# Cross-attention and mixture of experts on one core: experts as three float32r products, weights split by GpSimd into a ring of four, token rows scattered once

## The chip, the cores and the metric

One of the eight cores of a Trainium2 chip runs the whole program. A core has TensorE (PE; its weight loads are listed apart as PEld), VectorE (DVE), ScalarE (ACT), GpSimd (POOL), SyncE (SP), 16 DMA engines, SBUF with 128 partitions, and eight PSUM banks of 128 x 512 float32. The metric is the device time of one execution in microseconds, as the median of several runs. A granted clock of 1.0 is TensorE's 2.4 GHz, 0.5 its 1.2 GHz.

## The reference

There are 32 sequences of 64 tokens with 512 values each, all float32; the work goes by tiles of 128 tokens (two sequences), 16 of them.

```python
x = x + xattn(layernorm(x), ctx, ctx)   # autocorrelation attention, 8 heads, top 8 lags
x = x + moe(layernorm(x))

def moe(x):                             # per token
    g, u = split(x @ shared_w_gate_up.T)            # 512 -> 2 x 512
    shared = (silu(g) * u) @ shared_w_down.T        # 512 -> 512
    p = softmax(x @ gate_w.T)                       # 16 experts
    w, idx = top_k(p, 2);  w = w / sum(w)
    # every chosen expert: g, u = split(x @ w_gate_up[e].T)   512 -> 2 x 128
    #                      y_e  = (silu(g) * u) @ w_down[e].T 128 -> 512
    return sum_k w[k] * y_idx[k] + shared
```

A token goes to two experts, so there are 4096 pairs of token and expert. Each expert's pairs are filled up to whole tiles of 128 "slots". 47 tiles are always worked on, which is enough for any routing; those after the last filled one are done with expert 15.

## The kernel before, in words

Every engine has its own instruction stream, written out in order, and semaphores between them. In time order:

**Attention** (to about 203 us). Sixteen pairs of sequences go through a software pipeline: forward transforms as products with constant matrices (the context as three float32r products, `split_product`, L453), products, top lags, inverse, the sum into `resid`, the second normalisation `x2n`, its transposes, which are kept in `x2T`, and the gate's logits. SP loads `x` and `ctx` and stores `x2n` to DRAM (`x2_rows`, L405); every second pair it loads two experts' gate/up weights (`load_expert_pair`, L394), so that all of them stand in SBUF (`wgu_sb`).

**Routing and shared group 0** (to about 249 us). DVE ranks the logits and computes the slot of every pair (`pos_i`, L1043). To turn this into a list of tokens by slot (`slot_token`) and weights by slot (`slot_w`), DVE and GpSimd build one-hot matrices in eight turns (L1061 and L1235), and TensorE multiplies them (`slots`, L612). Between these, TensorE does group 0 (four token tiles) of the shared expert in float32 (`shared_half`, `shared_down`).

**The experts** (about 249 to 403 us). For slot tile `j`, GpSimd copies 128 indices and gathers 128 rows of `x2_rows` with an indirect DMA (`gather`, L1244). TensorE transposes them (L643), ScalarE copies them out of PSUM (L814), and TensorE multiplies by the expert's gate and up weights, in float32, at an address read from a table (L655): 128 x 256, four blocks. ScalarE takes the SiLU (L822), DVE multiplies with up and with the slot's weight (L1086), TensorE turns the activation (L664), DVE copies it (L1083), TensorE multiplies by the down weights (L670), DVE copies the result (L1091), and SP stores it to `y_rows` in DRAM. In iteration `j` TensorE's order is gate/up of `j`, transposes of `j+1`, the turn of `j-1`, the down product of `j-2`. The loops are hardware loops (`Fori`).

**Shared groups 1 to 3** (about 403 us to the end). Their operands are split in two float32r halves (`hi` by ScalarE, `lo` as the difference by DVE), and each product is done as hi x hi + hi x lo + lo x hi (`split_half`, L571; `split_down`, L586): 96 and 48 products of 512 columns per group. Meanwhile, once every `y` is stored (L1263), GpSimd gathers the results back by token: 16 tiles, two choices each, in four turns of eight buffers (`gather_results`, L1270). DVE adds them to `resid` (`add_results`, L1101), in one order with its multiplies and splits for TensorE, and adds the shared result (`shared_add`, L1007). A buffer is gathered into again when its last content has been added (`y_added`). SP stores each finished tile of `resid`.

Of the kernel before, what the change touches and what calls it, by code (L numbers as in the profile page):

```python
# [42 lines left out]
E = 16  # L43
# [5 lines left out]
JW = SLOT_TILES + 1  # L49
GROUPS = 4  # L50
# [5 lines left out]
HOTS = 4  # L56
HOT_TURNS = CHOICES * PAIRS // HOTS
# [84 lines left out]
def build(nc, x, ctx, consts, gate, w_gu, w_down, sh_gu, sh_down, out):  # L142
    with ExitStack() as stack:
# [3 lines left out]
        def in_turn(name, width, later):  # L147

            with nc.sbuf_tensor(name, [P, width], F32) as first:
                pass  # L150
            spare = width - sum(w for _, w, _ in later)
            tenants = [sb(n, [P, w], dt) for n, w, dt in later]
            if spare:
                sb(name + "_spare", [P, spare])
            return first, tenants
# [17 lines left out]
        x2_rows = nc.dram_tensor("x2_rows", [TOKENS, D], F32, kind="Internal").ap()  # L173
        y_rows = nc.dram_tensor("y_rows", [SLOT_TILES * P, D], F32, kind="Internal").ap()
# [4 lines left out]
        for name, width in CONSTANTS:  # L179
# [6 lines left out]
        wgu_sb, (y_in_low, shgu_hi, shgu_lo, tokens_hi, tokens_lo, act_lo) = in_turn("wgu_sb", E * KB * 2 * INTER, [  # L186
            ("y_in_low", YBUFS // 2 * D, F32), ("shgu_hi", KB * 2 * SHARED, F32R), ("shgu_lo", KB * 2 * SHARED, F32R),
            ("tokens_hi", GT * D, F32R), ("tokens_lo", GT * D, F32R), ("act_lo", SB * D, F32R)])
        shgu_sb = sb("shgu_sb", [P, KB * 2 * SHARED])
        gate_sb = sb("gate_sb", [P, KB * E])  # L190

        arena, (shd_hi, shd_lo, act_hi) = in_turn("arena", 21 * D, [
            ("shd_hi", SB * D, F32R), ("shd_lo", SB * D, F32R), ("act_hi", SB * D, F32R)])
        xg_sb = sb("xg_sb", [P, 2 * D])
        silu_sb = sb("silu_sb", [P, D])
        b_at = [0]
# [7 lines left out]
        ctx_halves = (act_lo[:, 0:D], act_lo[:, D:2 * D])  # L204
        matrices_halves = (act_lo[:, 2 * D:2 * D + 2 * P], act_lo[:, 2 * D + 2 * P:2 * D + 4 * P])
# [14 lines left out]
        wd_sb = arena[:, 0:E * D]  # L220
        shd_sb = arena[:, E * D:(E + SB) * D]
        totals = arena[:, (E + SB) * D:(E + SB) * D + E * PAIRS]
        cumul = arena[:, (E + SB) * D + E * PAIRS:(E + SB + 1) * D]


        EARLY_DOWN = (E - SB) * D
        sh_act = arena[:, EARLY_DOWN:EARLY_DOWN + SB * D]
# [7 lines left out]
        xgT = [x2T[:, 0:D], x2T[:, D:2 * D]]  # L235
        y_out = [x2T[:, 2 * D:3 * D], x2T[:, 3 * D:4 * D]]
        xg = [xg_sb[:, 0:D], xg_sb[:, D:2 * D]]
        act_sb = sb("act_sb", [P, P])
        actT_both = sb("actT_both", [P, 2 * P])
        actT_sb = [actT_both[:, 0:P], actT_both[:, P:2 * P]]  # L240

        y_in = [(y_in_low if i < YBUFS // 2 else x2T)[:, i % (YBUFS // 2) * D:(i % (YBUFS // 2) + 1) * D] for i in range(YBUFS)]
# [32 lines left out]
        hilo_i = sb("hilo_i", [P, CHOICES * PAIRS], I32)  # L275
        hi_f = sb("hi_f", [P, CHOICES * PAIRS])
        lo_f = sb("lo_f", [P, CHOICES * PAIRS])
        tile_e = sb("tile_e", [P, JW])

        tile_gu_at, tile_down_at = sb("tile_gu_at", [P, JW], I32), sb("tile_down_at", [P, JW], I32)  # L280

        lane_hot = [xg_sb[:, k * HOTS * P:(k + 1) * HOTS * P] for k in range(2)]
        tile_hot = [const_sb[:, k * HOTS * 2 * JW:(k + 1) * HOTS * 2 * JW] for k in range(2)]
        slot_token = sb("slot_token", [P, JW], I32)
        slot_w = sb("slot_w", [P, JW])
# [5 lines left out]
        ps_xgT, ps_gu, ps_y, ps_actT = bank[0], bank[6:8], bank[3:5], bank[5]  # L291
        ps_gate, ps_up, ps_shared = (bank[1], bank[7]), bank[2], (bank[0], bank[5], bank[3], bank[4])
        ps_slots, ps_rank, ps_total = bank[6], bank[3], bank[4]
# [4 lines left out]
        gate_loaded, wgu_loaded, shgu_loaded = sem("gate_loaded"), sem("wgu_loaded"), sem("shgu_loaded")  # L298
        wd_loaded, shd_loaded = sem("wd_loaded"), sem("shd_loaded")
# [24 lines left out]
        lane_hot_ready, tile_hot_ready = sem("lane_hot_ready"), sem("tile_hot_ready")  # L324
        slots_psum, slots_ready = sem("slots_psum"), sem("slots_ready")
        tile_hot_found = sem("tile_hot_found")
        tile_e_ready, pos_ready = sem("tile_e_ready"), sem("pos_ready")
# [5 lines left out]
        gidx_ready = sem("gidx_ready")  # L333
        gathered = [sem("gathered0"), sem("gathered1")]
        xgT_psum, xgT_ready, gu_psum, silu_ready = sem("xgT_psum"), sem("xgT_ready"), sem("gu_psum"), sem("silu_ready")
        act_ready, actT_psum, actT_ready = sem("act_ready"), sem("actT_psum"), sem("actT_ready")
        down_psum, y_ready = sem("down_psum"), sem("y_ready")
# [21 lines left out]
        WEIGHT_BLOCKS = [(i % 2, i // 2) for i in range(1, 2 * SB)] + [(0, 0)]  # L359
# [25 lines left out]
        def _(sp):  # L385
# [8 lines left out]
            def load_expert_pair(h):  # L394
                width = 2 * KB * 2 * INTER
                sp.dma_start(wgu_sb[:, bass.ds(h * width, width)],
                             w_gu[:, bass.ds(h * width, width)]).then_inc(wgu_loaded, 16)

            def iteration(h, b, n):
                if live(n, 2) and n != -2:  # L400
                    load_pair(h + 1, b)
                if live(n, -2):
                    p, pb = pair(h, b, -2)
                    sp.wait_ge(x2n_ready, p + 1)
                    sp.dma_start(x2_rows[bass.ds(p * P, P), :], x2n[pb]).then_inc(x2_stored[pb], 16)  # L405
                if n == 2:
                    sp.dma_start(shgu_sb[:, :], sh_gu[:, :]).then_inc(shgu_loaded, 16)
                if b == 1 and (n is None or 1 <= n < PAIRS):

                    wait(sp, wgu_loaded, 16 * h)  # L410
                    if n == PAIRS - 1:
                        sp.wait_ge(ctx_odd_psum, PAIRS)
                    load_expert_pair(h)
# [8 lines left out]
            sp.wait_ge(logits_psum, PAIRS)  # L422
            sp.wait_ge(x2T_kept, PAIRS)
            for b in range(2):
                sp.wait_ge(x2_stored[b], 16 * PAIRS // 2)
            sp.dma_start(shd_sb, sh_down[:, :]).then_inc(shd_loaded, 16)
            sp.dma_start(wd_sb[:, 0:EARLY_DOWN], w_down[:, 0:EARLY_DOWN]).then_inc(wd_loaded, 16)
            for t in range(GT):
                sp.wait_ge(sh_out_psum, t + 1)
                cols = slice(EARLY_DOWN + t * D, EARLY_DOWN + (t + 1) * D)  # L430
                sp.dma_start(wd_sb[:, cols], w_down[:, cols]).then_inc(wd_loaded, 16)

            def store_y(h, b):
                j = 2 * h + b
                sp.wait_ge(y_ready, j + 1)
                sp.dma_start(y_rows[bass.ds(j * P, P), :], y_out[b]).then_inc(y_stored[b], 16)

            with sp.Fori(0, SLOT_TILES // 2) as h:
                for b in range(2):
                    store_y(h, b)  # L440
# [873 lines left out]
```

## Time and profile before

| | |
|---|---|
| median of 3 runs | 509.45 us (509.12 to 509.93) |
| span of the profiled execution | 507.2 us |
| TensorE busy | 476.8 us (94%) |
| VectorE, ScalarE, GpSimd busy | 312.2, 222.7, 227.3 us |
| DMA | 66.76 MB, 132 GB/s over the span |

The only time of the profiled execution itself is its span, from its first to its last instruction; the runs' times hold in addition what lies around the span, and their median is 2.25 us above it. A busy time counts a matmul from its start to its modelled end, so neighbours overlap in it; the distance between starts tells the pace. The name behind an instruction is the tile that it writes, then those that it reads. "idle before, releaser" says how long an engine had nothing to do ahead of a group and what ended that.

### The profile page before, as it was taken

Reading aid. Unit: us, or ns where it says so; the run is one execution under the profiler, and the core shown is the slowest. Engines: PE = TensorE matmul, PEld = TensorE weight load, DVE = VectorE, ACT = ScalarE, POOL = GpSimd, SP = SyncE. Lnnn points to the kernel's source line nnn. Section 1 sums busy time; section 2 is a strip of 40 time slices with the busy share of each in tenths; the row PEclk is TensorE's granted clock in tenths of the full one; section 3 lists DMA queues with packets and bytes.
Section 4 is the critical chain, followed back from the end, with each engine's and each line's share of the span. In section 5 each row is a group of like instructions: output and inputs, shape, how many; then the busy total and the mean of one; then the engine's idle time right before and its main releaser. Section 6 shows DMA issues by size and latency. Waiting matters only on the chain.

```text
span 507.2 us, 8574 instructions
## 1 busy us (share of the span) xinstructions
PE 476.8 (94%) x2097; PEld 328.1 (65%) x2098; DVE 312.2 (62%) x972; ACT 222.7 (44%) x425; POOL 227.3 (45%) x384
## 2 busy tenths in 40 slices
PE   4789999999999999898899999999999999999997
PEld 2556556656655655356576667766667678888885
DVE  3799899999999863884133333333333566747643
ACT  4778888888888835200122222122221435022120
POOL 2356676676667544044333333333333026466520
PEclk9899999999999999999999999999999999999999
DMA  4416533424253031801435555455554314555622
GB/s 157 163 43 237 173 110 127 145 63 146 68 180 114 36 103 43 331 0 43 124 113 157 165 165 151 150 158 161 165 153 151 131 63 126 159 174 165 207 62 83
DMA packets 24923, 66.76 MB, mean 132 GB/s; under 512 B 3456, under 2 KB 3456, under 8 KB 23488
## 3 DMA queue, kind: packets, MB, share of 16 engines
q1 hardware_dynamic: 18576, 45.74, 25.0%
q0 software_dynamic: 6320, 20.71, 15.6%
q8 instruction: 11, 0.18, 0.1%
q14 instruction: 16, 0.13, 0.1%
HBM read 45.73 MB, written 20.71 MB: 131 GB/s over the span
## 4 chain that ended last, share of the span: by engine, by line
PE 62%; DVE 15%; POOL 8%; issue 8%; ACT 5%; DMA 1%; SPq 0%; DVEq 0%; POOLq 0%; ACTq 0%
PE bank L457 19%; PE bank L655 17%; PE bank L670 8%; PE bank L643 4%; DVE top_v L923 4%; POOL arena L1198 4%; PE bank L469 4%; POOL arena L1201 4%; PE bank L558 2%; DVE arena L928 2%; PE bank L567 2%; DVE stats L886 2%; DVE resid L911 2%; ACT arena L772 2%; ACT arena L771 2%
## 5 line engine op out<-in xcount | busy, mean ns | idle before, releaser
L655 PEld LDWEIGHTS bank<-wgu_sb,x2T 128*128 128x128 f32 x376 | 67.6, 189 | 41.0 <-issue 33.6
L655 PE MATMUL bank<-wgu_sb,x2T 128*128 x376 | 92.0, 388 | 2.1 <-ACT x2T L814 0.6
L814 ACT COPY x2T<-bank 128x512 f32<-128x512 f32 x47 | 27.5, 585 | 142.6 <-PE bank L643 142.6
L1251 POOL DMA_INDIRECT xg_sb<-x_rows,gidx x47 | 45.9, 976 | 98.0 <-PE bank L643 93.6
L1083 DVE COPY actT_both<-bank 128x128 f32<-128x128 f32 x47 | 13.7, 291 | 73.3 <-PE bank L664 73.3
L670 PE MATMUL bank<-arena,actT_both 128*128 x94 | 47.9, 593 | 0.0
L457 PE MATMUL bank<-act_lo 128*128 128x512 f32 x96 | 41.2, 538 | 6.7 <-DVE act_lo L965 6.7
L457 PE MATMUL bank<-tokens_hi,shgu_hi 128*128 128x512 f32 x92 | 36.2, 394 | 0.0
L457 PE MATMUL bank<-tokens_hi,shgu_lo 128*128 128x512 f32 x92 | 35.8, 389 | 0.0
L457 PE MATMUL bank<-tokens_lo,shgu_hi 128*128 128x512 f32 x92 | 35.8, 389 | 0.0
L457 PEld LDWEIGHTS bank<-act_lo 128*128 128x128 f32 x96 | 18.7, 197 | 22.8 <-issue 20.8
L558 PE MATMUL bank<-x2T,shgu_sb 128*128 128x512 f32 x72 | 32.6, 596 | 0.4 <-DVE arena L882 0.4
L1091 DVE COPY x2T<-bank 128x512 f32<-128x512 f32 x47 | 32.0, 680 | 0.8 <-PE bank L670 0.8
L1086 DVE SCALAR_TENSOR_TENSOR act_sb<-bank,slot_w,silu_sb 128x128 f32<-128x128 f32 x47 | 16.4, 350 | 23.8 <-ACT silu_sb L822 23.8
L643 PE MATMUL bank<-const_sb,xg_sb 128*128 128x128 f32 x188 | 28.3, 272 | 1.7 <-DMA xg_sb<-x_rows,gidx 1.7
L481 PE MATMUL bank<-const_sb,arena 128*128 128x128 f32 x128 | 26.0, 286 | 3.1 <-DVE arena L897 3.1
L1198 POOL TENSOR_TENSOR arena<-arena 128x512 f32<-128x512 f32 x16 | 20.5, 1284 | 18.1 <-ACT arena L772 18.1
L1201 POOL TENSOR_TENSOR arena<-arena 128x512 f32<-128x512 f32 x16 | 20.3, 1271 | 18.5 <-DVE arena L953 18.3
L481 PEld LDWEIGHTS bank<-const_sb,arena 128*128 128x128 f32 x128 | 21.5, 201 | 10.9 <-issue 7.8
L643 PEld LDWEIGHTS bank<-const_sb,xg_sb 128*128 128x128 f32 x188 | 23.5, 140 | 7.6 <-issue 3.1
L719 ACT ACTIVATE silu_sb<-bank 128x512 f32<-128x512 f32 x16 | 9.6, 598 | 40.1 <-PE bank L457 28.7
L882 DVE TENSOR_TENSOR arena<-bank,silu_sb 128x512 f32<-128x512 f32 x16 | 11.1, 691 | 26.0 <-PE bank L457 24.9
(153 smaller groups left out, 1077.7 us busy)
## 6 DMA issues: line engine op xcount, KB each, us to landing
y_rows<-x2T SPq DMA_DIRECT2D x47, 256.0 KB, 3.1
wgu_sb<-w_gu SPq DMA_DIRECT2D x8, 1024.0 KB, 5.3
resid<-x SPq DMA_DIRECT2D x16, 256.0 KB, 2.8
arena<-ctx SPq DMA_DIRECT2D x16, 256.0 KB, 3.3
x_rows<-arena SPq DMA_DIRECT2D x16, 256.0 KB, 2.1
result<-resid SPq DMA_DIRECT2D x16, 256.0 KB
arena<-w_down SPq DMA_DIRECT2D x1, 3072.0 KB, 13.0
shgu_sb<-sh_gu SPq DMA_DIRECT2D x1, 2048.0 KB, 8.0
```

The costliest lines, as they stand in the source:

```text
L457: last = mm(ps, a[i], b[k], start=start and n == 0, stop=stop and n == len(terms) - 1)
L469: mm(ps_out[:, :], C["out_odd"], odd_prod, start=False, stop=True).then_inc(out_psum, 1)
L481: mm(ps_corr[:, cols], prod_plain[:, cols], C["corr_plain"], start=True, stop=False)
L558: last = mm(ps[:, :].rearrange("p (t n) -> p t n", t=GT), shgu_sb[:, col:col + P], shared_tokens(g, c), start=c == 0, stop=c == KB - 1)
L643: last = nc.tensor.transpose(ps_xgT[:, cols], xg[b][:, cols], C["identity"])
L655: last = mm(ps_gu[b][:, 0:2 * INTER], xgT[b][:, c * P:(c + 1) * P], wgu_sb[:, bass.ds(at + c * 2 * INTER, 2 * INTER)], start=c == 0, stop= ...
L670: mm(ps_y[b][:, :], actT_sb[b], wd_sb[:, bass.ds(at, D)], start=True, stop=True).then_inc(down_psum, 1)
L814: copy(xgT[b], ps_xgT[:, :]).then_inc(xgT_ready, 1)
L1091: nc.vector.tensor_copy(y_out[b], ps_y[b][:, :]).then_inc(y_ready, 1)
L1198: nc.gpsimd.tensor_tensor(w_odd_sw, w_odd_sw, ctx_odd_im[pb], ALU.mult).then_inc(odd_im_products, 1)
L1201: nc.gpsimd.tensor_tensor(odd_prod, odd_prod, w_odd_sw, ALU.add).then_inc(odd_product_ready, 1)
L1251: nc.gpsimd.indirect_dma_start(xg[b], None, x2_rows[:, :], bass.IndirectOffsetOnAxis(ap=gidx[b][:, 0:1], axis=0)).then_inc(gathered[b], 16)
```

## The change

1. **Expert products in float32r.** The expert weights are one array now (gate/up and down of an expert side by side, 1536 columns). GpSimd loads one expert at a time into one of two raw buffers, copies it to a float32r `hi` and subtracts for `lo`, into one of four ring slots. `expert_split` counts the experts that are ready; a slot is used again when the tiles of the expert four before are done (`expert_tiles` against `expert_free`). Tokens by slot and activations are split too: `hi` by ScalarE, `lo` by DVE. Gate/up of a tile is 12 products of 256 columns, down three of 512. Transposes run two tiles ahead, into two banks; ScalarE copies the result `y`. The loops are written out.
2. **Rows are scattered once.** Instead of one-hot products and a gather per tile, SP loads the 16 tiles of `x2_rows` again, GpSimd scatters each twice by `pos_i` to a DRAM array in slot order (`x_slots`, 32 indirect DMAs), and SP loads a slot tile with a plain DMA. During attention SP fills `x_slots` with zeros (47 stores), since some slots stay empty. No slot tile is loaded, and no expert is split, before every scatter has landed.
3. **Order.** Shared group 1 is done before the experts; its weights' `lo` halves and its tokens' are GpSimd's work, ahead of the scatter, and ScalarE makes the `hi` halves between group 0's SiLUs. Four of the row buffers lie where `act_lo` will be, so DVE's first multiply of group 1 waits for their scatters. Group 2 starts behind the last tiles.
4. **Weights of the two choices** are applied when the results are added (`scalar_tensor_tensor`), and those additions stand elsewhere in DVE's order: the first turn after group 2's multiplies, the second with group 2's shared additions, the third in group 3's loop, the fourth behind it.

The core of the diff:

```diff
+            for t in range(PAIRS):                       # SP
+                if t == ROWS_LOW:
+                    sp.wait_ge(sh_up_psum, SB)
+                    sp.wait_ge(weights_lo_ready, 2 * SB)
+                if t >= ROWS_LOW + ROWS_HIGH:
+                    sp.wait_ge(rows_scattered[t - ROWS_HIGH], 16 * CHOICES)
+                sp.dma_start(row_buffer(t), x2_rows[t * P:(t + 1) * P, :]).then_inc(rows_loaded[t], 16)
...
+            for t in range(PAIRS):
+                sp.wait_ge(rows_scattered[t], 16 * CHOICES)
+            for j in range(SLOT_TILES + 6):
+                if j < SLOT_TILES:
+                    load_slots(j)
+                if j >= 6:
+                    store_y(j - 6)
...
+            def gate_up(j):                              # TensorE
+                at = weights_at(j)
+                need = pe.value_load(tile_need[0:1, j:j + 1], min_val=1, max_val=E)
+                pe.wait_ge(xgT_lo_ready, j + 1)
+                pe.wait_ge(expert_split, need)
+                for c in range(KB):
+                    last = split_product(ps_gu[j % 2][:, 0:2 * INTER],
+                                         of_halves(xgT_halves[j % 2], lambda x: x[:, c * P:(c + 1) * P]),
+                                         of_expert(at, c * 2 * INTER, 2 * INTER), c == 0, c == KB - 1)
+                last.then_inc(gu_psum, 1)
...
+            for j in range(SLOT_TILES):
+                gate_up(j)
+                if j + 2 < SLOT_TILES:
+                    transposes(j + 2)
...
+                if j >= 1:
+                    turn_act(j - 1)
+                if j >= 2:
+                    down(j - 2)
...
+            for t in range(PAIRS):                       # GpSimd
+                if t == PAIRS // 2:
+                    pool.wait_ge(sh_up_psum, SB)
+                    pool.wait_ge(tokens_lo_ready, GT)
+                    load_raw(0)
+                    load_raw(1)
+                pool.wait_ge(rows_loaded[t], 16)
+                for k in range(CHOICES):
+                    nc.gpsimd.indirect_dma_start(x_slots[:, :], bass.IndirectOffsetOnAxis(ap=pos_i[:, k * PAIRS + t:k * PAIRS + t + 1], axis=0),
+                                                 row_buffer(t), None).then_inc(rows_scattered[t], 16)
+
+            def split_expert(e):
+                pool.wait_ge(raw_loaded[e % 2], 16 * (e // 2 + 1))
+                hi, lo = (slot(e)[:, half * EXPERT:(half + 1) * EXPERT] for half in range(2))
+                nc.gpsimd.tensor_copy(hi, raw[e % 2]).then_inc(expert_hi, 1)
+                rest(lo, raw[e % 2], hi, expert_split, expert_hi, e + 1)
+                if e + 2 < E:
+                    pool.wait_ge(expert_split, e + 1)
+                    load_raw(e + 2)
...
+            for e in range(E):
+                if e == 2:
+                    pool.wait_ge(sh_out_psum, 2 * GT)
+                if e >= RING:
+                    pool.wait_ge(expert_tiles, pool.value_load(expert_free[0:1, e - RING:e - RING + 1], min_val=1, max_val=SLOT_TILES + 1))
+                    apart(pool, pool_passed)
+                split_expert(e)
...
+            slots_lo(0)                                  # DVE
+            slots_lo(1)
+            shared_add(1, 2)
+            shared_add(1, 3)
+            for j in range(SLOT_TILES):
+                expert_multiply(j)
+                if j + 2 < SLOT_TILES:
+                    slots_lo(j + 2)
+                if j >= 1:
+                    expert_act_lo(j - 1)
```

## Rows read from the trace of the kernel before

**Rows 1.** Busy time by stage: DMA share and GB/s last.
```profile
249.50:403.00 153.50, 151.35 (x694) 107.53 (x693) 56.44 (x138) 35.93 (x94) 50.87 (x87) 1.00 0.50 152
438.40:507.20 68.80, 65.40 (x289) 53.83 (x287) 36.44 (x55) 11.83 (x20) 29.11 (x45) 1.00 0.47 147
```
**Rows 2.** Timeline of TensorE: start, us, instruction; first gate/up, two tiles later on.
```profile
249.48 3.62 PE L655 MATMUL bank<-wgu_sb,x2T 128*128 x16
...
320.69 1.99 PE L655 MATMUL bank<-wgu_sb,x2T 128*128 x8
322.51 0.60 PE L643 MATMUL bank<-const_sb,xg_sb 128*128 128x128 f32 x4
322.95 0.27 PE L664 MATMUL bank<-const_sb,act_sb 128*128 128x128 f32 x1
323.06 1.02 PE L670 MATMUL bank<-arena,actT_both 128*128 x2
323.92 1.94 PE L655 MATMUL bank<-wgu_sb,x2T 128*128 x8
...
327.32 1.99 PE L655 MATMUL bank<-wgu_sb,x2T 128*128 x8
```
**Rows 3.** Timeline of TensorE, first and last of 48 float32r down products.
```profile
427.48 0.39 PE L457 MATMUL bank<-shd_hi,act_hi 128*128 128x512 f32 x1
...
438.13 0.39 PE L457 MATMUL bank<-shd_hi,act_lo 128*128 128x512 f32 x1
```
**Rows 4.** Timeline of TensorE, the logits: products of 16 columns.
```profile
177.97 0.96 PE L502 MATMUL bank<-gate_sb,xg_sb 128*128 128x16 f32 x8
```
**Rows 5.** Groups by form: busy us, mean ns of one, idle before them.
```profile
L814 ACT COPY x2T<-bank 128x512 f32<-128x512 f32 x47 | 27.5, 585 | 142.6 <-PE bank L643 142.6
L1229 POOL TENSOR_TENSOR act_lo<-arena,act_lo 128x512 fp32r<-128x512 f32 x15 | 19.0, 1268 | 12.2 <-ACT act_lo L739 12.2
L1192 POOL COPY x2T<-xg_sb 128x512 f32<-128x512 f32 x15 | 9.2, 614 | 0.0
```
**Rows 6.** Timeline of DVE: slot positions, and the last multiply of group 0.
```profile
216.44 0.18 DVE L1043 CAST pos_i<-pos_f 128x32 int32<-128x32 f32 x1
...
223.70 0.69 DVE L882 TENSOR_TENSOR arena<-bank,silu_sb 128x512 f32<-128x512 f32 x1
```
**Rows 7.** Timeline of GpSimd, gathers of results: first two, ninth, last of 32.
```profile
414.99 0.97 POOL L1280 DMA_INDIRECT y_in_low<-y_rows,gidx  x1 [3.08 <-issue]
...
416.98 0.97 POOL L1280 DMA_INDIRECT y_in_low<-y_rows,gidx  x1 [0.81 <-POOL gidx L1275]
...
435.26 1.24 POOL L1280 DMA_INDIRECT y_in_low<-y_rows,gidx  x1 [3.54 <-DVE resid L1112]
...
485.14 1.30 POOL L1280 DMA_INDIRECT x2T<-y_rows,gidx  x1 [0.83 <-POOL gidx L1275]
```
**Rows 8.** DMA queues: packets, MB, share; issues: count, KB, us to landing.
```profile
q1 hardware_dynamic: 18576, 45.74, 25.0%
q0 software_dynamic: 6320, 20.71, 15.6%
...
resid<-x SPq DMA_DIRECT2D x16, 256.0 KB, 2.8
...
xg_sb<-x_rows,gidx POOLq DMA_INDIRECT x47, 3.7
```
**Rows 9.** Busy time near the start; TensorE first, granted clock third from last.
```profile
16.00:18.00 2.00, 0.09 (x1) 0.00 (x0) 2.00 (x16) 1.96 (x5) 0.00 (x0) 1.00 0.42 95
18.00:20.00 2.00, 1.20 (x5) 1.21 (x6) 2.00 (x6) 1.94 (x5) 0.28 (x1) 0.68 1.06 400
20.00:22.00 2.00, 2.00 (x12) 2.00 (x11) 0.32 (x2) 0.47 (x1) 1.84 (x6) 0.50 0.70 274
```
**Rows 10.** Timeline of DVE: the last copied y, and the last sum.
```profile
408.94 0.69 DVE L1091 COPY x2T<-bank 128x512 f32<-128x512 f32 x1
...
503.84 0.69 DVE L1010 TENSOR_TENSOR resid<-bank,resid 128x512 f32<-128x512 f32 x1 [2.03 <-PE bank L457]
```

More of the change, by code:

```diff
@@ L49 @@
 JW = SLOT_TILES + 1
+RING = 4
+EXPERT = KB * 2 * INTER + D
+DOWN = KB * 2 * INTER
+SLOT = 2 * EXPERT
+ROWS_LOW, ROWS_HIGH = 4, 8
 GROUPS = 4
@@ L145, in sb, with over @@
             return stack.enter_context(nc.sbuf_tensor(name, shape, dt))
[L147 to L155, printed above, removed]
+        def over(tenants):
+            held = ExitStack()
+            made = [held.enter_context(nc.sbuf_tensor(n, [P, w], dt)) for n, w, dt in tenants]
+            held.close()
+            return made
         sems = {}
@@ L626, in _ @@
             shared_half(0, 3, 1)
[L627 removed]
             pe.wait_ge(shd_loaded, 16)
             shared_down(0, 0)
[L630 removed]
             shared_down(0, 1)
[L632 to L640 removed]
+            pe.wait_ge(pos_ready, 1)
+            shared_down(0, 2)
+            shared_down(0, 3)
@@ L641, in transposes @@
+            for i, (part, m) in enumerate(WEIGHT_BLOCKS):
+                pe.wait_ge(weights_lo_ready, i + 1)
+                split_half(1, m, part)
+            def transposes(j):
+                pe.wait_ge(xg_loaded[j % 2], 16 * (j // 2 + 1))
+                wait(pe, xgT_lo_ready, j - 1)
                 for c in range(KB):
                     cols = slice(c * P, (c + 1) * P)
-                    last = nc.tensor.transpose(ps_xgT[:, cols], xg[b][:, cols], C["identity"])
+                    last = nc.tensor.transpose(ps_xgT[j % 2][:, cols], xg[j % 2][:, cols], C["identity"])
@@ L699, in _, with weights_at, of_expert @@
-            pe.wait_ge(weights_lo_ready, len(WEIGHT_BLOCKS) + SB)
-            pe.wait_ge(xgT_ready, SLOT_TILES)
-            pe.wait_ge(actT_ready, SLOT_TILES)
-            pe.wait_ge(y_ready, SLOT_TILES)
-            split_down(1)
-            with pe.Fori(2, GROUPS) as g:
+            def weights_at(j):
+                return pe.value_load(tile_at[0:1, j:j + 1], min_val=0, max_val=(RING - 1) * SLOT)
+            def of_expert(at, first, width):
+                return tuple(ring[:, bass.ds(at + (half * EXPERT + first), width)] for half in range(2))
@@ L1093, in _ @@
-            for n in range(2):
-                expert(0, n, n)
-            with dve.Fori(1, SLOT_TILES // 2) as h:
-                for b in range(2):
-                    expert(h, b, None)
-            expert(SLOT_TILES // 2, 0, SLOT_TILES - 1)
             def add_results(quad, u):
@@ L1167, in _ @@
                 split_act_lo(3, m)
-                add_results(3, m)
+                add_results(2, m)
+            for t in range(GT):
+                add_results(3, t)
             dve.wait_ge(y_added, PAIRS)
@@ L1254, in _, with rest @@
-            pool.wait_ge(slots_ready, 1)
-            for b in range(2):
-                pool.wait_ge(x2_stored[b], 16 * PAIRS // 2)
-                gather(0, b)
-            with pool.Fori(1, SLOT_TILES // 2) as h:
-                for b in range(2):
-                    gather(h, b)
-            gather(SLOT_TILES // 2, 0)
+            def rest(dst, src, hi, done, hi_ready, value):
+                pool.wait_ge(hi_ready, value)
+                nc.gpsimd.tensor_tensor(dst, src, hi.bitcast(F32), ALU.subtract).then_inc(done, 1)
```

496 lines of the change are left out of this document (219 added, 277 removed).

## The prediction

> **What bounds the kernel now.** I read the stages first, then one expert tile, then the three resources that the change leans on: GpSimd, the DMA engines, and what follows the last expert tile. In the stage of the experts TensorE is busy for 151 of 153.5 us and in the last stage for 65.4 of 68.8 [rows 1]; the other engines are at a third or less, DMA at about half. So both stages are bound by TensorE. A tile starts every (327.32 - 320.69)/2 = 3.32 us [rows 2]: 1.82 for the eight gate/up instructions, 0.44 for four transposes, 0.11 for turning the activation, 0.86 for the down product; that is 3.23, and the rest is a pause ahead of every second tile, where the gate/up waits for ScalarE's copy of the transposes made just before it. The end of the kernel is a TensorE chain too: DVE's last sum starts at 503.84 and runs 0.69, and 2.7 us of storing later the span is over [rows 10]. GpSimd's 32 gathers of results run beside it from 414.99 to 485.14 [rows 7] and cost nothing now.
>
> **Expert products.** A float32r product of 512 columns starts every (438.13 - 427.48)/47 = 0.227 us [rows 3]. No 256-column one is in the trace. Half of that, 0.113, is its lower bound (what an instruction costs besides its columns can only add), the full 0.227 its upper one. A weight load with a 16-column product behind it takes at most 0.96/8 = 0.12 [rows 4], so the load alone sets about the same floor, and I take 0.12. Gate/up is then 12 x 0.12 = 1.44, down 3 x 0.227 = 0.68, the transposes stay at 0.44 and 0.11: 2.67. Transposes now run two tiles ahead, which removes the pause; I leave 0.05 for the rest: 2.72 a tile, with ends of 2.64 and 4.0. For the 47 tiles TensorE needs 47 x 1.49 + 45 x 0.44 + 46 x 0.11 + 45 x 0.68 = 125.5 us, then two group-2 halves of 12 x 0.227 and the two last downs, 6.9, and ScalarE's copy of the last result, 0.6 [rows 5]: the last y stands 133.0 us after the first gate/up.
>
> What must keep up with 2.72: ScalarE has 2 x 0.585 for transposes and y [rows 5] and two narrower operations, at most as much again: 2.34. GpSimd splits an expert in 3 x 0.614 + 3 x 1.268 = 5.65, issues one load and waits a little: 6.9, or 7.7 if an issue costs 1.8. The inputs' routing, counted from the reference, fills 42 of the 47 tiles, so an expert lasts 42/16 x 2.72 = 7.1; with a ring of four and the last seven or eight tiles all at expert 15, even 7.7 delays the end by 2 us at most. DMA moves two 256 KB blocks a tile at 126.8/45.74 us per MB (the q1 row, 0.73 a block) and 0.79 MB of weights per expert, 0.83 a tile [rows 8]: 2.28 of 2.72, tight but within.
>
> **What goes before the experts.** The 32 one-hot products between the downs go, their DVE and GpSimd halves too, and so do the 47 gathers by GpSimd. pos_ready still comes at 216.6, the last up of group 0 is read from 223.7, its activation stands at 224.4 [rows 6]; four downs of four 0.86 products [rows 2] then end group 0 at 238.2, where the experts start at 249.5 now. Group 1 follows at once: 96 products of 0.227 to 260.0, plus 1.4 for a new wait (DVE's first multiply of the group stands behind the landing of four scattered tiles at about 247, and the up of block 1 waits for it), then 24 more: 266.8. Here TensorE runs dry, because the experts wait for the scatter. GpSimd splits the shared weights and tokens first: the tokens wait for that last up and a ScalarE copy of 0.6, to 224.1, and eight subtractions of 1.268 end at 234.3. Then 32 scatters and two loads are queued on it, and every expert split stands behind them. One issue costs at least its own 0.97 and at most 0.97 + 0.83, for each gather now starts 0.81 to 0.83 after what released it [rows 7]. I take that the 0.83 passes beside the issue before, since a scatter, other than a gather, waits for no index copy. Then DMA decides: a software-queue DMA holds all 16 engines for 79.1/79 = 1.0 us [rows 8], so 32 scatters, four row tiles (2.9) and two raw experts (4.4) need 39.3 us, 1.16 an issue. From 235.1 they are issued by 274.4, and landed 2.7 later (3.7 from issue to landing), at 277.1. SP's first slot load takes 2.8, as its x tiles do [rows 8]: 279.9. TensorE has then been idle for 13 us. Near the start, after two microseconds with 0.09 busy, the granted clock was 0.68 and then 0.50 (the lower of its two levels, 1.2 of 2.4 GHz) in stretches of 2 us [rows 9]; I take the loss of those, 0.64 + 1.0 = 1.7. Two transposes and 24 products are 6.3: the first gate/up at 287.9. Expert 0 is split by 277.1 + 5.7, earlier. So the experts start 38.4 us later, and of these only 144 x 0.227 = 32.7 are group 1, done ahead: the hole eats more than the dropped one-hots gave.
>
> **What comes after.** The last y stands at 287.9 + 133.0 = 420.9, against 408.94 + 0.69 = 409.63 now. So the loop gives 27.1 and the last y is still 11.3 later. Groups 2 and 3 alone would let TensorE end at 480 (288 x 0.227 from 413.4, and 1.5 for the last tiles). But the gathers start only when every y is stored: 5.36 after the last y [rows 7, 10], at 426.3. Their code is unchanged: 70.15 us from the first issue to the last, 3.54 of it a wait that won't recur, so 66.6, to 492.9, and 3.7 to land: 496.6. What was hidden becomes the end. DVE adds one result (0.7) and four shared sums (2.5), and 2.7 us of storing follow the last one [rows 10]: 502.5. From the last y to the end it is 81.6 us instead of 97.6. On the way TensorE waits for DVE, because the group-3 multiply stands behind the additions of the second turn of gathers (to about 463); that is inside the gathers' time and costs nothing.
>
> **Other edits.** 47 zero stores (34 us of DMA time) replace eight weight loads of 1 MB (23) over the 180 us of attention, where DMA is busy for under half: nothing, at most a late context tile or two, 0 to 5. Routing steps cut on DVE: 2 us, not on the path. ScalarE's splits of the shared weights between SiLUs: under group 0's products. Weights applied in the last additions instead of per tile: the additions keep their 0.7.
>
> **Sum.** Span 507.2 - 4.7 = 502.5. The median of the runs is 509.45, 2.25 above the profiled span; so 504.8.
>
> **A rule against it.** The Trainium skill, "TensorE: Matmul & The Clock Gate", Part 3, has LDWEIGHTS overlapping a running matmul only where the row groups differ. Rows 3 speak against that: load and 512 columns together take 0.227. At 256 columns it is the third rival below.
>
> **The rivals.** *Issues at 1.8* (ends slower): if the 0.83 can't overlap, 34 issues take 61.2, the landing is at 299.0 instead of 277.1, and all behind it moves: 526.7 with the 2.25. It decides from 1.30 us an issue on, where the 4.7 are gone. For it: every gather shows it. Against: what stands before each gather is a dependent copy. *The tile is not cheaper*: 256-column products at 0.16, because of register-addressed operands, late slot loads at 84% DMA or the splits' pace, give 3.2 a tile, +22.5: 527. For it: no such product has run; against: float32 instructions of 256 columns take half of those of 512. *Loads in series with the products*: 0.12 + 0.113 each, +1.36 a tile, +64: 569. *Cheaper queue*: scatters at 0.97 and DMA no limit (-5), the 3.08 us before the first gather gone: 497. *Gathers don't bind*: only if they sped up by a third; TensorE sets the end, 480 + 3.4 + 2.25: 486.
>
> **How the numbers follow.** Forecast 0.45 (own range 500 to 510), issues at 1.8 0.21, dear tile 0.17, loads in series 0.03, cheaper queue 0.10, gathers that don't bind 0.04. About 0.2% is what a measurement can tell, 508.4 to 510.5. Faster: 0.36 of the 0.45, 0.10 and 0.04, together 0.50. Same: 0.06. Slower: the rest, 0.44. For eight in ten I go from the cheaper queue, 494, to the two rivals at 527, 529.
>
> **What would show it.** Right: gate/up groups of about 1.45 us at 2.7 us a tile; a hole in TensorE from about 267 to 280, released by a slot load, with the lower clock behind it; first gate/up near 288; gathers some 2.06 us apart as the last chain, with TensorE done over 10 us before the end. Wrong: scatters 1.8 apart; tiles above 3 us; the chain at the end on TensorE; expert_split as what releases the gate/up.

## The result: 562.3 us, slower by 10.2%

The changed kernel takes 562.26 us (median of 4 runs, 559.76 to 564.59), the kernel before 509.69 beside it (4 runs): a ratio of 1.102 [1.097, 1.106]. The forecast was 504.8, the range 494 to 529: outside it, and on the other side of no change. The profiled span is 562.8 us against a forecast span of 502.5, 60.3 more. That execution took 564.6 us, 2.3 above the median. Two runs of the experiments below fell into a slower state (683.5 us without reads, 504.0 with one load for two tiles): the ratios leave them out, and the medians without them are 519.9 and 498.9. Three marks of the trace divide these 60.3:

| mark | forecast | measured | of it new here |
|---|---|---|---|
| first gate/up starts | 287.9 | 294.82 | +6.9 |
| last y copied (from the first gate/up on) | 420.9 (133.0) | 478.45 (183.6) | +50.6 |
| end (from the last y on) | 502.5 (81.6) | 562.8 (84.4) | +2.8 |

So five sixths of the miss lie inside the expert loop. The first mark itself moves between executions: in the kernels below whose start is unedited it lies between 292.6 and 294.8, so of the +6.9 some 2 are spread.

### The profile after, stage by stage

Busy time of the two last stages, which answers [rows 1]: the expert tiles up to the last copied y, then the rest.

```profile
294.80:478.45 183.65, 150.28 (x961) 124.44 (x960) 55.57 (x141) 75.46 (x188) 77.03 (x42) 0.99 0.53 184
478.45:562.80 84.35, 61.38 (x262) 49.98 (x260) 40.88 (x59) 11.03 (x20) 42.81 (x64) 0.88 0.50 153
```

TensorE, the first engine in the row, was busy for 151.35 of 153.5 us in the experts before; now it is busy for 150.3 of 183.7, at full clock (0.99), and no other engine comes to half (the DMA engines' share is 0.53). Something that is not a listed instruction fills 33 us.

One tile, which answers [rows 2]: the timeline of all engines from a down product to the next gate/up.

```profile
402.34 0.72 PE L467 MATMUL bank<-ring,actT_hi 128*128 x2
...
402.90 0.39 PE L467 MATMUL bank<-ring,actT_lo 128*128 x1
...
403.11 0.69 DVE L1095 TENSOR_TENSOR xgT_lo<-bank,xgT_hi 128x512 fp32r<-128x512 f32 x1 [0.46 <-ACT xgT_hi L835]
...
404.01 0.32 PEld L467 LDWEIGHTS bank<-ring,xgT_hi 128*128 128x128 f32 x2 [1.14 <-issue]
404.01 0.51 PE L467 MATMUL bank<-ring,xgT_hi 128*128 x2 [0.73 <-DVE xgT_lo L1095]
...
404.36 0.28 PE L467 MATMUL bank<-ring,xgT_lo 128*128 x1
...
404.72 0.28 PE L467 MATMUL bank<-ring,xgT_lo 128*128 x1
```

The previous gate/up started at 400.30, so a tile takes 3.7 here and 3.80 on average over three (the next starts are 407.85 and 411.69), not 2.72. From 404.36 to 404.72 there are three products: 0.12 each, as forecast. The down products start 0.23 to 0.28 apart; 402.90 is the third, and behind it the next product was due at 403.13. What is new is the 0.88 from 403.13 to 404.01. The row of PE puts the wait down to DVE's `xgT_lo`, and so does the chain of waits (start, us, what):

```profile
402.01 0.45 PE bank L652 x4
402.46 0.02 issue
402.49 0.60 ACT xgT_hi L835
403.08 0.02 issue
403.11 0.70 DVE xgT_lo L1095
403.81 0.20 issue
404.01 1.71 PE bank L467 x12
```

This is theory C (chain): transposes, ScalarE's half, VectorE's rest, next gate/up. But the code speaks against it. The rest that DVE makes at 403.11 is for the transposes of 402.01, two tiles ahead; the gate/up of 404.01 needs the one that was made a tile earlier. The row of the weight loads says something else: 1.14 of "issue", time in which nothing that the profile shows was waited for. The trace also has what TensorE's own sequencer did meanwhile: the register instructions of its stream, listed as PEldq under the lines that read registers (ns as min/median/max, then first and last start). A read is a load of a register from a table in SBUF, an operation on it and an assertion that it lies within its bounds. L656 is the place of the weights, L664 the count of split experts:

```profile
L656 PEldq TENSOR_LOAD <-tile_at x1: 301/301/301, 402.5 to 402.5; - x1
L656 PEldq FUSED_REGOPS  x1: 151/151/151, 402.8 to 402.8; - x1
L656 PEldq SEQ_ASSERT  x1: 18/18/18, 403.1 to 403.1; - x1
...
L664 PEldq TENSOR_LOAD <-tile_need x1: 297/297/297, 403.1 to 403.1; - x1
L664 PEldq FUSED_REGOPS  x1: 151/151/151, 403.5 to 403.5; - x1
L664 PEldq SEQ_ASSERT  x1: 18/18/18, 403.7 to 403.7; - x1
```

The two reads run one after the other from 402.5 to 403.7, 0.6 us each with the steps between; a third, for the down product, stands at 401.5. Meanwhile only down products that stand ahead of them in the stream still start (the last at 402.90), and gate/up starts right behind them. This is theory R (reads): 1.8 us a tile on the sequencer, with only 2.7 us of products to cover them.

The start of the experts, which answers the bounds from [rows 7] and the clock of [rows 9]: GpSimd's second, third and last scatter (the first stands at 238.98), and then TensorE.

```profile
240.51 0.97 POOL L1248 DMA_INDIRECT x_slots<-rows_low,pos_i  x1 [0.30 <-issue]
241.79 0.96 POOL L1248 DMA_INDIRECT x_slots<-rows_low,pos_i  x1 [0.30 <-issue]
...
281.34 0.96 POOL L1248 DMA_INDIRECT x_slots<-shgu_sb,pos_i  x1 [0.31 <-issue]
```

```profile
286.70 1.97 PE L652 MATMUL bank<-const_sb,x2T 128*128 128x128 f32 x8 [15.24 <-DMA x2T<-x_slots]
...
288.89 0.63 PE L467 MATMUL bank<-shd_lo,act_hi 128*128 128x512 f32 x1
289.31 0.63 PE L467 MATMUL bank<-shd_hi,act_lo 128*128 128x512 f32 x1
...
294.82 0.40 PE L467 MATMUL bank<-ring,xgT_hi 128*128 x2
```

Most scatters stand 1.27 to 1.28 apart. TensorE stands idle for 15.24 us, released by a slot load, and its products are then 0.42 apart instead of 0.23, the lower of its two clocks, until 290.2 (granted clock 0.50 up to 290, 1.00 from 291).

The end, which answers [rows 7, 10]: first, ninth and the last two gathers of results, then the last two lines of DVE.

```profile
481.54 1.03 POOL L1285 DMA_INDIRECT x2T<-y_rows,gidx  x1 [0.83 <-POOL gidx L1280]
...
501.06 0.98 POOL L1285 DMA_INDIRECT x2T<-y_rows,gidx  x1 [4.00 <-DVE resid L1091]
...
550.13 0.98 POOL L1285 DMA_INDIRECT x2T<-y_rows,gidx  x1 [0.81 <-POOL gidx L1280]
...
552.12 1.15 POOL L1285 DMA_INDIRECT x2T<-y_rows,gidx  x1 [0.81 <-POOL gidx L1280]
```

```profile
555.79 0.75 DVE L1091 SCALAR_TENSOR_TENSOR resid<-x2T,r_w,resid 128x512 f32<-128x512 f32 x1 [1.58 <-DMA x2T<-y_rows,gidx]
556.58 2.48 DVE L1029 TENSOR_TENSOR resid<-bank,resid 128x512 f32<-128x512 f32 x4
```

The last chain runs over the gathers, 2.0 apart, as forecast; TensorE's last product is done near 548.5.

### The profile page after: what moved, and what is told of

It reads as the page before. It is cut to its first block, busy times and chain, and to the rows that moved or that the text cites. A ratio compares the mean times of both kernels' runs of the same rounds, so it can differ in the third digit from the quotient of the medians.

```text
span 562.8 us, 8677 instructions
## 1 busy us (share of the span) xinstructions
PE 465.2 (83%) x2272; PEld 336.3 (60%) x2272; DVE 296.5 (53%) x937; ACT 262.4 (47%) x519; POOL 302.7 (54%) x371
## 4 chain that ended last, share of the span: by engine, by line
PE 33%; POOL 19%; DVE 18%; issue 14%; ACT 9%; DMA 5%; SPq 1%; POOLq 1%; DVEq 0%; ACTq 0%
PE bank L467 20%; POOL x_slots L1248 5%; DVE xgT_lo L1095 5%; ACT xgT_hi L835 4%; POOL x2T L1285 4%; PE bank L652 4%; PE bank L568 4%; DVE top_v L942 3%; POOL arena L1183 3%; POOL arena L1186 3%; PE bank L479 3%; DMA resid<-x 2%; DVE arena L947 2%; DVE stats L905 2%; DVE resid L930 2%
## 5 line engine op out<-in xcount | busy, mean ns | idle before, releaser
L467 PE MATMUL bank<-ring,xgT_hi 128*128 x376 | 75.3, 298 | 31.4 <-DVE xgT_lo L1095 30.6
L467 PEld LDWEIGHTS bank<-ring,xgT_hi 128*128 128x128 f32 x376 | 59.4, 192 | 50.2 <-issue 50.0
L1223 POOL TENSOR_TENSOR ring<-x2T,ring 128x1536 fp32r<-128x1536 f32 x16 | 55.5, 3470 | 1.4
L467 PE MATMUL bank<-ring,xgT_lo 128*128 x188 | 53.6, 285 | 0.0
L1095 DVE TENSOR_TENSOR xgT_lo<-bank,xgT_hi 128x512 fp32r<-128x512 f32 x47 | 32.5, 692 | 38.4 <-ACT xgT_hi L835 38.4
L1285 POOL DMA_INDIRECT x2T<-y_rows,gidx x32 | 34.9, 1091 | 29.7 <-POOL gidx L1280 23.0
L652 PE MATMUL bank<-const_sb,x2T 128*128 128x128 f32 x188 | 29.4, 281 | 16.2 <-DMA x2T<-x_slots 16.2
L835 ACT CAST xgT_hi<-bank 128x512 fp32r<-128x512 f32 x47 | 27.6, 587 | 27.2 <-PE bank L652 27.2
L467 PEld LDWEIGHTS bank<-ring,xgT_lo 128*128 128x128 f32 x188 | 36.3, 193 | 0.0
L467 PE MATMUL bank<-ring,actT_hi 128*128 x94 | 33.9, 442 | 1.0 <-issue 0.8
L652 PEld LDWEIGHTS bank<-const_sb,x2T 128*128 128x128 f32 x188 | 22.6, 145 | 16.8 <-DMA x2T<-x_slots 16.8
```

Of the source, the lines that this page charges most:

```text
L467: last = mm(ps, a[i], b[k], start=start and n == 0, stop=stop and n == len(terms) - 1)
L652: last = nc.tensor.transpose(ps_xgT[j % 2][:, cols], xg[j % 2][:, cols], C["identity"])
L835: copy(xgT_halves[j % 2][0], ps_xgT[j % 2][:, :]).then_inc(xgT_hi_ready, 1)
L1095: tt(dst, src, hi.bitcast(F32), ALU.subtract).then_inc(done, 1)
L1223: nc.gpsimd.tensor_tensor(dst, src, hi.bitcast(F32), ALU.subtract).then_inc(done, 1)
L1285: nc.gpsimd.indirect_dma_start(y_in[buf], None, y_rows[:, :], bass.IndirectOffsetOnAxis(ap=gidx[buf][:, 0:1], axis=0)).then_inc(y_gathered ...
```

## The experiments

All are edits of the changed kernel. The first two write this input's routing into the program, and half the scatter leaves out the rows of the second choices, which only a diagnosis may do. "Loop" is the time from the first gate/up to the last copied y.

| kernel | us | ratio to before | loop |
|---|---|---|---|
| changed kernel | 562.3 | 1.102 [1.097, 1.106] | 183.6 |
| count known | 542.3 | 1.065 [1.062, 1.068] | 162.9 |
| no reads | 520.2 | 1.019 [1.016, 1.022] | 140.3 |
| read early, place used twice | 532.8 | 1.047 [1.043, 1.050] | 151.3 |
| four tiles a read, unbounded | 655.6 | 1.288 [1.283, 1.293] | 276.3 |
| four tiles a read, bounded | 547.3 | 1.076 [1.071, 1.081] | 169.2 |
| one read a tile | 525.8 | 1.033 [1.027, 1.039] | 146.2 |
| direct gathers | 543.0 | 1.066 [1.062, 1.071] | 183.7 |
| half the scatter | 552.3 | 1.083 [1.079, 1.087] | 184.0 |
| one read and direct gathers | 506.8 | 0.994 [0.992, 0.996] | 145.8 |
| the same, late downs first | 502.9 | 0.986 [0.984, 0.988] | 148.4 |
| the same, one load for two tiles | 499.4 | 0.979 [0.975, 0.982] | 142.7 |

### Which waits fill the loop: the count known, no reads

```diff
-                need = pe.value_load(tile_need[0:1, j:j + 1], min_val=1, max_val=E)
+                need = TILE_EXPERT[j] + 1
```

> The count of split experts that a tile waits for is written into the program; the place of the weights is still read, twice a tile. Theory R (reads): TensorE's sequencer spends about 0.6 us on each of its three register reads of a tile (0.30 load, 0.15 register operation, 0.02 assertion and the steps between), and in float32r there is not enough queued work ahead of them. One read of three goes: the loop falls from 3.80 us a tile to about 3.2, 47 x 0.6 = 28 us less, about 534 us. Theory C (chain: transposes, ScalarE's rounded half, VectorE's rest, next gate and up, as the chain of waits shows it): nothing changes, 3.80 us a tile and 562 us.

542.3 us, loop 162.9: 20.8 less, 0.44 a tile. C, which expects no change, falls. R had 0.6 a tile and 534 us: it missed by 8, as if part of the read was covered.

```diff
-                return pe.value_load(tile_at[0:1, j:j + 1], min_val=0, max_val=(RING - 1) * SLOT)
+                return TILE_EXPERT[j] % RING * SLOT
```

> Place and count are both written into the program; TensorE reads no register at all in the loop, and the products, the waits on the data and all other engines stay. Theory R: the loop falls to the 2.72 us a tile that the products need, or up to 2.85 with the waits: 47 x 0.95 to 1.08 = 45 to 51 us less, 511 to 517 us. Theory C: the chain over ScalarE and VectorE stays as long as it is, 3.80 us a tile and 562 us.

The count is a constant here too, and with the place the address of every weight product becomes one: the operation of 0.046 us on the sequencer that makes such an address (shown with the four-tile reads below) goes as well. 520.2 us, loop 140.3: 43.3 less than in the changed kernel, with ScalarE's and VectorE's part untouched. That the reads are what counts, and not the address operations, shows in the last run below: it keeps these, and its loop takes 142.7. TensorE's timeline, three tiles on end, and its waits in the loop (us in total, times, longest):

```profile
399.38 0.40 PE L470 MATMUL bank<-ring,xgT_hi 128*128 128x256 f32 x2
...
402.07 0.40 PE L470 MATMUL bank<-ring,xgT_hi 128*128 128x256 f32 x2
...
404.75 0.39 PE L470 MATMUL bank<-ring,xgT_hi 128*128 128x256 f32 x2
```

```profile
PE bank L655 <- DMA x2T<-x_slots: 7.0, 10, 1.3
```

A tile takes 2.68: the forecast's 2.72 is what the products need once the reads are gone. All that is left of TensorE's waits are ten for slot loads, 7.0 us, which are the 7.3 by which this loop exceeds the forecast 133.0. They can account for the 3 us by which the time ends above R's 511 to 517.

### Place or number of the reads: early, and in one instruction

```diff
             for j in range(SLOT_TILES):
                 gate_up(j)
+                if j + 1 < SLOT_TILES:
+                    read(j + 1)                  # place and count of the next tile
...
             def down(j):
-                at = weights_at(j)
+                at, _ = places.pop(j)            # the register that gate_up used
```

> The two reads for tile j+1 stand right behind the products of gate and up of tile j, ahead of the transposes, and the down product uses the register that gate and up used, so two reads a tile instead of three. Theory R, with the sequencer as the serial resource: the third read goes and the place of the other two does not matter: about 3.2 us a tile, 28 us less, 534 us. Theory R, with only the place at fault (nothing queued behind which to read): 2.72 to 2.85 us a tile, 511 to 517 us. Theory C: 562 us.

532.8 us, loop 151.3: far from what place alone would give (511 to 517), near the serial version (534). But the kernel with the count known also reads twice a tile, and its loop takes 162.9; so the place counts too, by 0.25 us a tile, and neither version holds alone. The number of reads is the larger part: the two that are left still cost 11.0 us beside none.

```diff
+            def read(j, n=4):                    # in gate_up, every fourth tile
+                load = lambda table, **bounds: nc.values_load_multi_w_load_instructions(table[0:1, j:j + n], ..., **bounds)[1]
+                tables = (load(tile_at, skip_runtime_bounds_check_because=...), load(tile_need, min_val=1, max_val=E))
```

> One instruction reads the places of four tiles, one the counts of four tiles; the down product uses the place again. Theory R: two loads of 0.30 and four register operations with assertions of about 0.17 for every four tiles, about 0.4 us a tile instead of 1.8, part of it covered: 2.75 to 3.1 us a tile, 33 to 49 us less, 513 to 529 us. Theory C: 562 us.

655.6 us, 93 more where 33 to 49 less were expected: both theories wrong here, the edit had a cost of its own. The sequencer's rows on the products' line, 40 us of the loop:

```profile
L467 PEldq FUSED_REGOPS  x137: 42/146/168, 381.9 to 420.0; - x137
L467 PEldq SEQ_ASSERT  x102: 18/18/18, 382.1 to 419.5; - x102
```

In the changed kernel the address of a weight product cost an operation of 0.046 and no assertion (from 400 to 408 us):

```profile
L467 PEldq FUSED_REGOPS  x23: 46/46/51, 400.2 to 408.0; - x23
```

Here, where the place was read without bounds, it costs 0.146 and an assertion at every use. With bounds:

> As the kernel that reads four tiles at once, which took 655 us, but the places are read with bounds. Theory: there the trace has a register operation of 0.15 and an assertion of 0.02 for the address of every weight product instead of an operation of 0.046, because a value without bounds is asserted at each use; with bounds these go and the eight assertions for four tiles come in one piece, about 2.0 us for every four tiles: 2.9 to 3.2 us a tile, 520 to 535 us. Rival: one instruction that fills four registers is itself slow: it stays near 655 us.

547.3 us, loop 169.2, 107 less: bounds were the cause. It missed 520 to 535 by 12. The eight operations of four tiles come in one piece: nine waits of TensorE whose only releaser in the profile is "issue" hold 18.1 us in the loop, the longest 2.2. And the granted clock is lower, 0.92 on average between 300 and 420 against 0.99 in the changed kernel (0.50 from 306 to 308, behind a pause of 1.82). The shares of the two were not separated.

```diff
+                need, at = nc.values_load_multi_w_load_instructions(tile_pair[0:1, 2 * j:2 * j + 2], ..., min_val=1, ...)[1]
+                places[j] = at - 1, need         # the table holds the place plus one
```

> Place and count of a tile lie side by side in one table; one instruction reads both, behind the products of gate and up of the tile before, and the down product uses the place again. The run with two reads a tile took 3.1 us a tile, the one with none 2.68 between its stalls. If the reads are all that is left: one load of 0.30 and two register operations with assertion of about 0.2, 0.7 us a tile instead of 1.2, nearly all of it covered by what is queued: 2.7 to 2.9 us a tile, 512 to 522 us. Rival: what is left is the register arithmetic of each weight address (12 to 13 operations of 0.046 a tile), which this kernel keeps: about 3.1 us a tile, 530 us.

525.8 us, a tile 3.0, between theory and rival. The rows of the read, over the whole loop:

```profile
L659 PEldq FUSED_REGOPS  x94: 151/151/165, 289.5 to 427.6; - x94
L659 PEldq SEQ_ASSERT  x94: 18/18/28, 289.7 to 427.8; - x94
L659 PEldq TENSOR_LOAD <-tile_pair x47: 532/537/725, 288.7 to 426.6; - x47
```

A load of two registers takes 0.54, not the 0.30 that I had put in; with two operations the read fills 1.1 us a tile. That the rest is not the address arithmetic shows in the last run below, which keeps it. The runs spread from 524.3 to 529.9.

### The start and the end

```diff
-                for k in range(CHOICES):
+                for k in range(CHOICES - 1):
                     nc.gpsimd.indirect_dma_start(x_slots[:, :], ...)
```

> Only the rows of the first choices are scattered; the second choices' slots stay zero, and the rest of the program runs on them as before. If the scatter sets the start of the experts one to one: 16 x 1.27 = 20 us are taken out, of which TensorE's 15.2 us hole at 271.3 can give back 13 to 15: first gate and up near 281, 547 to 550 us. Rival: the first expert's weights or the slots' zeroing set the start: the hole closes by less than 5 us and the time stays above 557 us.

552.3 us. First gate/up at 282.04, 12.8 earlier, first gather 12.4, end of the span 11.8: the scatter sets the start of the experts and all behind it moves along. The medians differ by 9.9 and the expected 547 to 550 was missed by 2: the start came 12.8 earlier, not 13 to 15.

```diff
-                    nc.gpsimd.tensor_copy(gidx[buf][:, :], pos[:, k, bass.ds(t, 1)]).then_inc(yidx_ready, 1)
-                    pool.wait_ge(yidx_ready, turn * YBUFS + buf + 1)
...
+                    nc.gpsimd.indirect_dma_start(y_in[buf], None, y_rows[:, :],
+                        bass.IndirectOffsetOnAxis(ap=pos_i[:, k * PAIRS + t:k * PAIRS + t + 1], axis=0)).then_inc(y_gathered[buf], 16)
...
                 split_act_lo(2, m)               # DVE, group 2
+                if m:
+                    add_results(0, m - 1)
```

> The expert loop stays as it is (3.80 us a tile). The results are gathered with the columns of the position table as offsets, without a copy of each column and the wait on it, and VectorE adds the first results between the steps of the third group of shared tokens instead of behind them. If GpSimd's gathers bind the end (2.0 us each, and 8.7 us in which TensorE waits for VectorE behind them): the pace falls to that of the scatters, 1.27 us, until TensorE's own 66 us behind the loop bind: 15 to 20 us less, 542 to 547 us. Rival: the gathers go at the pace at which their rows land, and the copies were hidden: 555 to 562 us.

543.0 us, as the theory has it; the two edits, on GpSimd and on DVE, were not run apart. The first twelve gathers now go at about the scatters' pace (later ones wait up to 3.23 us for DVE's additions), and TensorE no longer waits behind the loop (windows of 10 us, TensorE busy first):

```profile
479.95 0.97 POOL L1281 DMA_INDIRECT x2T<-y_rows,pos_i  x1 [0.30 <-issue]
481.22 0.96 POOL L1281 DMA_INDIRECT x2T<-y_rows,pos_i  x1 [0.31 <-issue]
```

```profile
504.00:514.00 10.00, 10.00 (x46) 8.29 (x45) 6.65 (x11) 1.82 (x3) 7.87 (x8) 1.00 0.88 275
514.00:524.00 10.00, 10.00 (x46) 8.29 (x45) 5.50 (x8) 2.44 (x4) 3.81 (x5) 1.00 0.55 176
```

In the changed kernel TensorE waited here for DVE's first multiply of group 3:

```profile
521.84 0.79 PE L467 MATMUL bank<-tokens_hi,shgu_hi 128*128 128x512 f32 x1 [8.66 <-DVE sh_act L901]
```

### Put together

> The one read a tile and the direct gathers with VectorE's new order, together. They took 36 and 19 us from the changed kernel (562.3 to 525.8 and to 543.0), one in the loop and one behind it. If both sit on the one path that sets the end, they add up: 562.3 - 36.4 - 19.3 = 506.6 us, 0.5 to 1% below the kernel before. Rival: with an earlier end of the loop something else behind it binds (TensorE's 66 us there were already without a gap in the direct gathers' run, so the loop's gain has to pass through whole; if not, the results' stores or the first gathers wait): 512 us or more.

506.8 us for 506.6: the two gains add up, as closely as runs that spread from 504.0 to 509.0 can tell.

```diff
             split_down_early(1)
+            split_down_late(1, 2)
+            split_down_late(1, 3)
             pe.wait_ge(tables_ready, 1)
```

> The same, and the last two down products of the second group of shared tokens (24 products, 288.2 to 294.8 in the changed kernel) stand ahead of the first slots' transposes, where TensorE waits 15 us for the scatter. If only their place behind the hole held the experts up: the first gate and up comes when the first slot's halves are ready, near 290.0 instead of 294.8, 4 to 5 us less than the run without it: 502 us. Rival: the first expert's split on GpSimd (to 289.4) or the second slot's halves hold the start, and the clock, lower after the hole, then slows gate and up instead: within 2 us of the run without it.

502.9 us, 3.9 less. First gate/up at 289.86, 5.0 earlier; now the first expert's split holds it, for 0.91:

```profile
286.98 1.97 PE L653 MATMUL bank<-const_sb,x2T 128*128 128x128 f32 x8 [9.80 <-DMA x2T<-x_slots]
289.86 0.79 PE L468 MATMUL bank<-ring,xgT_hi 128*128 x2 [0.91 <-POOL ring L1231]
```

The loop is 2.6 longer: the granted clock stays at 0.50 until 294 (until 291 without the edit), and now it is the first gate/up that runs at it. So the theory gives the start, and the rival's clock takes half of it back: in the two profiled executions the last y stands 2.4 earlier.

```diff
+                pair = nc.values_load_multi_w_load_instructions(tile_pair[0:1, 2 * j:2 * j + 4], ...)[1]     # every second tile
+                for i in range(2):
+                    need, at = pair[2 * i:2 * i + 2]
+                    places[j + i] = (nc.s_assert_within(at, 0, (RING - 1) * SLOT, skip_runtime_bounds_check_because=...),
+                                     nc.s_assert_within(need, 1, E))
```

> As the kernel with both and the late downs (502.9 us), but one load of four registers serves two tiles, and of each tile only the count is asserted; the places, multiples of a slot's size from the program's own table, are not. In the run with one read a tile the load of two registers took 0.54, not 0.30, and with two register operations of 0.15 and their assertions the reads filled 1.1 us a tile; a load of four took 0.33 in the kernel that reads for four. Theory R: 0.33 + 2 x 0.25 = 0.83 for two tiles, 0.4 a tile, nearly all covered: 2.72 to 2.85 us a tile instead of 3.0, first gate and up to last result 139 to 142 us instead of 148.4, 494 to 497 us. Rival: the loop already stands on the slot loads (7.0 us of waits for them came up in the run without reads): 501 to 503 us.

499.4 us, 2.1% [1.8, 2.5] under the kernel before. The load of four registers, and TensorE's waits in the loop:

```profile
L659 PEldq TENSOR_LOAD <-tile_pair x24: 328/337/883, 287.1 to 419.9; - x24
```

```profile
PE bank L653 <- DMA x2T<-x_slots: 5.9, 8, 1.1
PE bank L468 <- POOL ring L1235: 1.0, 1, 1.0
PE bank L653 <- issue: 0.4, 1, 0.4
```

The reads are covered (0.4 of issue left), a tile takes 2.7 where no slot load is late, and what remains is the 5.9 for slot loads, as in the run without reads. Theory R and the rival each hold a part: the time came 2 us above 494 to 497 with these waits in it. What makes those loads late (DMA's mean share was 0.73 in this loop) I did not test; it stays open.

## Why the prediction was wrong

**The step that failed is "I leave 0.05 for the rest: 2.72 a tile".** It adds up TensorE's instructions and forgets what its sequencer does for a tile. The change adds a third register read and a wait on it, and my part on the change does not price them. Measured: 3.80 a tile; without reads 2.68. Of the 50.6 us by which the loop missed, 43.3 are the reads (shown by taking them out; the address operations that went with them are in the last run's loop of 142.7, so they are not the cause), 7.0 slot loads that come late once the loop is fast. For those I had "2.28 of 2.72, tight but within".

The trace of the kernel before had the price, under its own reading line, which I did not open:

```profile
L647 PEldq FUSED_REGOPS  x157: 42/151/165, 248.1 to 404.2; - x157
L647 PEldq SEQ_ASSERT  x94: 18/18/24, 248.4 to 404.4; - x94
L647 PEldq TENSOR_LOAD <-tile_gu_at x47: 297/702/775, 247.6 to 399.0; - x47
L647 PEldq TENSOR_LOAD <-tile_down_at x47: 296/301/316, 254.9 to 403.8; - x47
```

Two reads a tile there too, and they cost little: TensorE had 2.15 us of idle time in that whole stage [rows 1], with 3.23 us of products in a tile to cover the reads [rows 2]. The pause of 0.2 us ahead of every second tile, which I put down to ScalarE's copy, may itself be a read: ahead of the gate/up of 327.32 the copy and the read's assertion both end at 327.0, and which of them held it stays open. The change shortened the cover by half a microsecond and made two reads three. The third read is not the whole of it: with the count known two reads a tile were left, and the loop still took 22.6 us more than without any. The Trainium skill, "DMA: Bandwidth & Descriptors", section "Latency and other measured facts", puts a floor of some 600 ns under a tensor_load and has the compiler unroll by four to make up for it. The loads of one register in the changed kernel took 0.30, under that floor, and the measurement decides; 0.6 is what a read takes with its operation and its assertion. That one load can serve several agrees: four registers took 0.33.

**The products: right.** 0.12 for 256 columns, 0.23 for the down. With that *loads in series* falls, and with it the rule in Part 3 of the Trainium skill's "TensorE: Matmul & The Clock Gate" as I had applied it. Its time, 569, lies nearer to the result than any other number of the prediction, for a reason that is not there. *The tile is not cheaper* had named register-addressed operands, but as 0.16 for each product; the products kept 0.12, and the cost is one per tile.

**The scatter: right in its size, not in what sets it.** 1.27 an issue, between 1.16 and the 1.8 of the rival; the gap between issues is 0.30, so most of the 0.83 falls away, as I took it. But it is not DMA that decides, with the 1.16 I had for it: the scatters wait for nothing but "issue", 0.96 and 0.30, at a DMA share of 0.69 over their stretch, and the direct gathers have the same pace. Late by 3.9 at its start (238.98 for 235.1), because the last up product of group 0 came late and with it GpSimd's first subtraction for the tokens (228.92 for 224.1), and by 4.0 over its length, less 1.0 made up between the last issue and the first gate/up: the +6.9. Hole, releaser and low clock behind it are as forecast.

**The end: right.** 84.4 for 81.6: the gathers take 4.0 more and what follows them 1.1, but the first comes 3.1 after the last y and not 5.4. The gathers bind, 2.0 apart, and TensorE waits for DVE inside their time. One sub-step was wrong: the wait of 3.54 ahead of the second turn did recur, as 4.00, because the first additions still stand behind group 2's operands on DVE. And "costs nothing" for TensorE's wait held only as long as the gathers were slow: with direct gathers it would have been next, which is argued and not run, since that run reorders DVE as well.

## What to carry to other kernels

When an edit shortens an engine's instructions, add up what its sequencer does per iteration as well: register reads, their assertions, address operations. In the kernel before they were nearly free under the products of a tile, the cover that the edit made shorter; the profile lists them under the line that reads, not among the busy times. And where a wait is put down to the last semaphore to come, check in the code whether the waiting instruction needs that one: here it named a chain that had nothing to do with it.

## What was unexpected of the hardware

- A register load took 0.30 us for one register, 0.54 for two and 0.33 for four. Why two are dearer than four stays open, as does the 0.70 of the kernel before's gate/up read.
- A register value without bounds is asserted at each use: 0.146 and 0.018 for each weight address, instead of 0.046. The loops of the two kernels that read four at a time differ by 107 us, in this and in what comes with it (granted clock 0.85 against 0.92 between 300 and 420).
- Indirect DMAs without a copied index follow each other at 1.27 us where nothing else holds them, in either direction; with it, at 2.0.
